# Gated cross-attention with routed experts on one core: stacks by single loads, softmax sums and reciprocals sent from GpSimd's program

## The reference

```python
# B = 8 batches, 256 tokens, 512 features, 32 query heads in 8 groups, head dim 16
q = X @ Wq.T + bq ; k = ctx @ Wk.T + bk ; v = ctx @ Wv.T + bv      # X = layernorm(x)
scores = einsum('bgrqd,bgkd->bgrqk', q, k) / sqrt(16)
scores = where(causal | padding, -inf, scores)
w = softmax(scores, axis=-1)
out = einsum('bgrqk,bgkd->bgrqd', w, v) ... @ Wo.T + bo
x = x + tanh(g_xattn) * out
# then a mixture of 8 experts (top 2 by a sigmoid gate + bias) and a shared expert:
x = x + tanh(g_ffn) * moe(layernorm(x))
```

## Time and profile before

| | before |
|---|---|
| device time, median of 3 runs | 839.02 us (834.45 to 839.38) |
| the profiled execution | 838.73 us; from first to last instruction (span) 836.8 us |
| PE busy | 695.0 us (83% of the span), 4417 matmuls |
| DVE / ACT / POOL busy | 452.3 / 290.4 / 109.3 us |
| mean granted TensorE clock | 0.884 of full |
| expert phase | from 648 us to the end |
| length of one full pass | about 68.3 us |

### The profile page before, as it was taken

The page is one execution under the profiler, slowest core; times in us unless marked ns, Lnnn a source line. Parts: engine busy times, 40 slices in busy tenths (PEclk is TensorE's granted clock), DMA queues, the critical chain, the costliest instruction groups (busy, mean ns, idle before and its releaser), DMA issues. The chain is left out here.

```text
span 836.8 us, 15086 instructions
## 1 busy us (share of the span) xinstructions
PE 695.0 (83%) x4417; PEld 481.2 (58%) x4417; DVE 452.3 (54%) x1017; ACT 290.4 (35%) x601; POOL 109.3 (13%) x132
## 2 busy tenths in 40 slices
PE   0345999899699799969979979989447999999998
PEld 0344757577477577758757758557236444444443
DVE  4517674467467556745736746634223455555554
ACT  1020454344344443433524434434210333333332
POOL 7400002102101210210210210110230000000000
PEclk9965978899899988988988989859667999999999
DMA  4785565455444643733644533421326012222211
GB/s 152 162 241 111 111 139 139 92 122 139 104 113 117 146 104 83 162 75 91 173 85 113 138 101 80 103 57 42 102 63 127 22 46 61 63 63 63 63 44 44
DMA packets 67696, 84.85 MB, mean 101 GB/s; under 512 B 15624, under 2 KB 44112, under 8 KB 67408
## 3 DMA queue, kind: packets, MB, share of 16 engines
q1 hardware_dynamic: 63504, 77.58, 36.4%
q0 software_dynamic: 2304, 6.29, 4.0%
q10 hardware_dynamic: 1856, 0.57, 0.3%
HBM read 60.48 MB, written 29.70 MB: 108 GB/s over the span
## 5 line engine op out<-in xcount | busy, mean ns | idle before, releaser
L623 ACT ACTIVATE probs<-ps 128x512 f32<-128x512 f32 x256 | 146.5, 598 | 153.1 <-PE ps L957 152.8
L831 DVE TENSOR_REDUCE mx<-ps 128x2 f32<-128x512 f32 x256 | 171.5, 683 | 47.2 <-PE ps L938 46.8
L1106 PE MATMUL ps_h<-w,q_sg 128*128 128x512 bf16 x512 | 132.9, 383 | 5.2 <-PEq L77 5.2
L938 PE MATMUL ps<-kst,qst 65*128 65x256 f32 x512 | 125.6, 331 | 12.9 <-DVE mx L831 7.7
L938 PEld LDWEIGHTS ps<-kst,qst 65*128 65x128 f32 x512 | 95.8, 211 | 61.9 <-issue 24.6
L957 PE MATMUL ps<-qst,kst 66*128 66x512 f32 x256 | 114.8, 450 | 5.2 <-DMA qst<-mrow 3.9
L1157 DVE SCALAR_TENSOR_TENSOR hid<-ps_h,sc_in,up 128x256 bf16<-128x256 f32 x128 | 61.9, 483 | 87.3 <-ACT up L1147 86.3
L1147 ACT ACTIVATE up<-ps_h,sc_in 128x256 f32<-128x256 f32 x128 | 60.7, 475 | 120.2 <-PE ps_h L1106 119.6
L1106 PEld LDWEIGHTS ps_h<-w,q_sg 128*128 128x128 bf16 x512 | 49.9, 99 | 67.8 <-issue 10.6
L970 PE MATMUL psa<-probs,v_st 128*32 128x256 f32 x1024 | 78.9, 432 | 1.2 <-ACT probs L623 1.2
L1124 PE MATMUL ps_o<-probs,hidT 128*128 128x512 bf16 x256 | 76.2, 380 | 0.8 <-DVE hidT L1163 0.8
(11 more groups left out here) (126 smaller groups left out, 1132.2 us busy)
## 6 DMA issues: line engine op xcount, KB each, us to landing
qst<-q_d SPq DMA_DIRECT2D x96, 128.0 KB
q_d<-q_sg SPq DMA_DIRECT2D x32, 256.0 KB, 2.2
a_d<-a_sb SPq DMA_DIRECT2D x32, 256.0 KB, 2.2
x_n<-in_x SPq DMA_DIRECT2D x8, 512.0 KB, 4.3
c_raw<-in_ctxT SPq DMA_DIRECT2D x8, 512.0 KB, 3.3
w<-in_w13T POOLq DMA_DIRECT2D x8, 512.0 KB, 16.0
a_dn<-a_d SPq DMA_DIRECT2D x16, 256.0 KB
a_lo<-r_d SPq DMA_DIRECT2D x16, 256.0 KB
```

The costliest lines, as they stand in the source:

```text
L623: act.activation(probs[:, v % 8, :], ps2[v % 2][:, :, :].rearrange("p h q -> p (h q)"), ACT.Exp, scale=HD ** -0.5).then_inc(s_exp, 1)
L831: dve.tensor_reduce(mx[:, c % 2, 0:8 * NT].rearrange("p (h t) -> p h t", t=NT)[:, h:h + 2, w // 2], ps1[u % 2][:, :, :], AX_X, ALU.max)\
L938: last = pe.matmul(o[:, i, :], qst[0:ROW_MAX, c, h, t * P:t * P + P], kst[0:ROW_MAX, c, g % 2, :], start=(i == 0 or not masked), stop=not ...
L1106: last = pe.matmul(o, xb[:, t, c, :], w13[:, e, c, :], start=(c == 0), stop=(c == DC - 1))
```

## The change

Single loads: `q_d` and `k_d` hold three rows per feature (hi, lo, hi and hi, hi, lo) and the padding row lies in `k_d`, so that each stack takes one load for q and one for k where it took seven; in turn each store becomes two, with half as many bytes again. Sums: `move_sums`, `store_r` and `load_r` are taken out of SP's program and issued from POOL's, in places of POOL's order; `normalise(b-1, 1)` goes ahead of `values(b+1, 0)`, and `residual_bias` ahead of `values(b, 3)`. Steps: Q1, Q2, Q3 move from 16, 18, 20 to 17, 20, 22, V0 and V1 from 21, 22 to 25, 26, and the second reciprocal with `load_values` from 20 to 19.

```diff
-PREP = [(11, "T0"), (12, "T1"), (13, "K"), (14, "Q0"), (16, "Q1"), (18, "Q2"), (20, "Q3"), (21, "V0"), (22, "V1")]
+PREP = [(11, "T0"), (12, "T1"), (13, "K"), (14, "Q0"), (17, "Q1"), (20, "Q2"), (22, "Q3"), (25, "V0"), (26, "V1")]
...
-        q_d = dram("q_d", (B, CH, P, 2, L))
-        k_d = dram("k_d", (B, P, 2, L))
-        pad_d = dram("pad_d", (B, L))
+        q_d = dram("q_d", (B, CH, P, 3, L))
+        k_d = dram("k_d", (B, G, HD + 1, 3, L))
...
             def store_k(nb, idx):
                 ready((s_free, idx["K"] + 1))
-                sp.dma_start(k_d[nb], f(k_sg[:, :, :])).then_inc(s_kw, 16)
+                kv = k_d[nb, :, 0:HD].rearrange("s d w q -> s d (w q)")
+                sp.dma_start(kv[:, :, 0:L], f(k_sg[:, hi, :])).then_inc(s_kw, 16)
+                sp.dma_start(kv[:, :, L:3 * L], f(k_sg[:, :, :])).then_inc(s_kw, 16)
...
-                sp.dma_start(q_d[nb, c], f(q_sg[:, c % 2])).then_inc(s_qw[c % 2], 16)
+                sp.dma_start(q_d[nb, c, :, 0:2], f(q_sg[:, c % 2])).then_inc(s_qw[c % 2], 16)
+                sp.dma_start(q_d[nb, c, :, 2], f(q_sg[:, c % 2, hi])).then_inc(s_qw[c % 2], 16)
...
-                for row, w in ((0, hi), (HD, lo), (2 * HD, hi)):
-                    sp.dma_start(f(qs[row:row + HD]), qv[w]).then_inc(s_stk[c], 16)
-                for row, w in ((0, hi), (HD, hi), (2 * HD, lo)):
-                    sp.dma_start(f(ks[row:row + HD]), kv[w]).then_inc(s_stk[c], 16)
-                sp.dma_start(f(ks[ROW_PAD:ROW_PAD + 1]), pad_d[bass.ds(nb, 1)].unsqueeze(1).broadcast_to([1, 2, L]))\
+                sp.dma_start(f(qst[0:ROW_PAD, c]), q_d[nb, c].rearrange("(s d) w q -> (d w) s q", d=HD))\
+                  .then_inc(s_stk[c], 16)
+                sp.dma_start(f(kst[0:ROW_PAD + 1, c]),
+                             k_d[nb, 2 * c:2 * c + 2].rearrange("s d w q -> (d w) s q")[0:ROW_PAD + 1])\
                   .then_inc(s_stk[c], 16)
...
             def body(b, attn, nxt, prev, old, base, par0):          # GpSimd's program
                 idx, _, at = numbered(attn, nxt, prev, old, base)
+                if prev:
+                    move_sums(b - 1, 1)
+                    store_r(b - 1, 0)
+                    load_r(b - 1, 0)
                 if attn:
                     values(b, 2, None)
+                if prev:
+                    move_sums(b - 1, 2)
                 if nxt:
                     deviation1(b + 1)
                 if prev:
                     normalise(b - 1, 0)
                     low_values(b - 1, 0)
+                if prev:
+                    residual_bias(b - 1)
                 if attn:
                     values(b, 3, None)
                 if prev:
-                    residual_bias(b - 1)
+                    move_sums(b - 1, 3)
+                    store_r(b - 1, 1)
+                    load_r(b - 1, 1)
+                    normalise(b - 1, 1)
+                    low_values(b - 1, 1)
+                if attn:
+                    move_sums(b, 0)
                 if nxt:
                     values(b + 1, 0, idx)
                 if prev:
-                    normalise(b - 1, 1)
-                    low_values(b - 1, 1)
                     deviation2(b - 1, 0)
                     deviation2(b - 1, 1)
...
-                    if u in (4, 20) and prev:
-                        h = u // 20
+                    if u in (4, 19) and prev:
+                        h = u // 19
```

More of the change, by code:

```diff
@@ L348, in store_a @@
                              a_sb[:, c % 2]).then_inc(s_aw[c % 2], 16)
-            def move_sums(b, c):
-                ready((s_aev, b * G + 2 * c + 2), (s_rd, b * 2 + c // 2 - 1))
-                for w in range(2):
-                    row = 32 * c + 16 * w
-                    sp.dma_start(den[row:row + 16, :], a_sb[HD:P:32, c % 2, w, :]).then_inc(s_den[c % 2], 16)
             def load_values(b, h):
@@ L363, in load_values @@
                              a_d[b, :, 0:HD, 2 * L * h:2 * L * h + 2 * L]).then_inc(s_ar[h], 16)
-            def store_r(b, h):
-                ready((s_rd, b * 2 + h + 1))
-                for i in range(2):
-                    c = 2 * h + i
-                    sp.dma_start(r_d[b, h, :, L * i:L * i + L], rden[32 * c:32 * c + 32, :]).then_inc(s_rw, 16)
-            def load_r(b, h):
-                ready((s_rw, b * 64 + 32 * h + 32), (s_ln2, b * LN2))
-                sp.dma_start(f(a_lo[:, 2 * h:2 * h + 2, :].rearrange("p c q -> p (c q)")),
-                             r_d[b, h].unsqueeze(1).broadcast_to([G, HD, 2 * L])).then_inc(s_rr[h], 16)
             def load_residual(b):
@@ L427, in body @@
                         c = {1: 1, 8: 2, 17: 3}[u]
-                        move_sums(b - 1, c)
                         store_a(b - 1, c)
@@ L442, in body @@
                         load_stack(b, 3)
-                    if prev and u in (5, 20):
-                        load_values(b - 1, u // 20)
-                    if prev and u in (5, 21):
-                        store_r(b - 1, u // 21)
-                    if prev and u in (9, 23):
-                        load_r(b - 1, u // 23)
+                    if prev and u in (5, 19):
+                        load_values(b - 1, u // 19)
                     if u == 17 and attn:
                         max_row(b, 1, idx)
-                    if nxt and u in (15, 17, 19, 21):
-                        store_q(b + 1, (u - 15) // 2, idx)
+                    if nxt and u in (15, 18, 21, 23):
+                        store_q(b + 1, {15: 0, 18: 1, 21: 2, 23: 3}[u], idx)
                     if nxt and u == 22:
@@ L455, in body @@
                     if attn and u == 24:
-                        move_sums(b, 0)
                         store_a(b, 0)
@@ L463, in _ @@
             passes(sp, body, prepare)
-            for s, n in ((s_kw, 16 * B), (s_rw, 64 * B),
-                         (s_qw[0], 32 * B), (s_qw[1], 32 * B), (s_aw[0], 32 * B), (s_aw[1], 32 * B)):
+            for s, n in ((s_kw, 32 * B),
+                         (s_qw[0], 64 * B), (s_qw[1], 64 * B), (s_aw[0], 32 * B), (s_aw[1], 32 * B)):
                 sp.wait_ge(s, n)
@@ L496, in values, with move_sums, store_r, load_r @@
                     .then_inc(s_vst, 1)
+            def move_sums(b, c):
+                ready((s_aev, b * G + 2 * c + 2), (s_rd, b * 2 + c // 2 - 1))
+                for w in range(2):
+                    row = 32 * c + 16 * w
+                    pool.dma_start(den[row:row + 16, :], a_sb[HD:P:32, c % 2, w, :]).then_inc(s_den[c % 2], 16)
+            def store_r(b, h):
+                ready((s_rd, b * 2 + h + 1))
+                for i in range(2):
+                    c = 2 * h + i
+                    pool.dma_start(r_d[b, h, :, L * i:L * i + L], rden[32 * c:32 * c + 32, :]).then_inc(s_rw, 16)
+            def load_r(b, h):
+                ready((s_rw, b * 64 + 32 * h + 32), (s_ln2, b * LN2))
+                pool.dma_start(a_lo[:, 2 * h:2 * h + 2, :].rearrange("p c q -> p (c q)").bitcast(F32),
+                             r_d[b, h].unsqueeze(1).broadcast_to([G, HD, 2 * L])).then_inc(s_rr[h], 16)
             def normalise(b, h):
@@ L558, in _ @@
             passes(pool, body, prepare)
+            pool.wait_ge(s_rw, 64 * B)
             pool.wait_ge(s_w13, 16 * E)
@@ L597, in item @@
                     act.wait_ge(s_item, n + 1)
-                    wait(act, s_qw[1], b * 32)
+                    wait(act, s_qw[1], b * 64)
                     act.activation(k_sg[:, hi, :], m[:, 0:L], ACT.Identity, bias=bk_c[:, 0:1]).then_inc(s_khi, 1)
@@ L602, in item @@
                     act.wait_ge(s_item, n + 1)
-                    wait(act, s_qw[c % 2], b * 32 + 16 * (c // 2))
+                    wait(act, s_qw[c % 2], b * 64 + 32 * (c // 2))
                     if c == 1:
-                        act.wait_ge(s_kw, b * 16 + 16)
+                        act.wait_ge(s_kw, b * 32 + 32)
                     act.activation(q_sg[:, c % 2, hi, :], m[:, 0:L], ACT.Identity, bias=bq_c[:, c:c + 1])\
```

11 lines of the change are left out of this document (4 added, 7 removed).

## The result

The changed kernel takes 858.08 us (median of 4 runs, 856.51 to 862.94) beside 839.2 us before: a ratio of 1.0246, 95% interval 1.0189 to 1.0304. It is slower by 19 us where 27 us less were forecast, and 26 us above the upper end of the range. The profiled execution's span is 857.4 us (before: 836.8), the mean granted clock 0.875 (before: 0.884).

A forecast was written before the change was run, and what follows sets the result against it. PE was taken to bound the pass, with idle time and lost clock at W0 to win. From 838.7 us, 28 off for five full passes, 2.4 off for the start and 3.6 added for the drain gave 811.9, forecast 812; range 788 to 832.

The forecast's parts named there:

- PE's way to W0: Full passes: PE reaches W0 at 220 to 221, where it came at 221.2, leaving a wait of 2 to 3 us.
- A new wait earlier in the pass: norm1 on DVE waits 1.5 us for POOL's deviation1, now behind chunk 2's sums; 0.8 us a pass reaches PE (0 to 1.5).
- Single loads in the passes: Full passes: they free SP of 20 issues a pass and add five; worth nothing, as PE waited for no stack.
- The start: Before the first scores: two issues replace seven, so the first stack's issues end 2.7 us sooner; 2.4 us won (0 to 2.7).
- The chain: Second half's sums to W0 in a full pass: 16.3 us (14.5 to 17.8) in place of 21.4, W0 4.3 us earlier.
- The price of a hop from POOL: Each of the chain's three transfers costs 0.6 us more from POOL than from SP (bounds 0 and 1.1).
- The clock at W0: Half of W0's 2.56 us lost to half speed comes back with the shorter wait: 1.3 us per full pass.
- Rival B: Hops cost 1.1 us and W0 still runs at half speed: 827 us; chance 0.14.
- The drain: After the last pass: sums leave 2.8 us later, store_r 1.8 later, three hops at 0.6; 3.6 us lost (1.8 to 5.1).
- The slower side: Chance 0.06 that the changed kernel is slower; with hops 2.5 us dearer than SP's it would take 853 us.
- Rival D: DVE's stops at norm1 and the reciprocal bring PE to W0 4 us later; only clock is won: 827 or 833 us; chance 0.13.
- The forecast's list of signs: Wrong if POOL's hops land over 1.7 us later, row-maxima waits exceed 2 us a pass, or a stack is waited for.

The follow-up runs named there:

- a4_dev: The changed kernel with deviation1 moved ahead of chunk 2's sums in POOL's order: 840.5 us, ratio 1.0052 to the kernel before.
- d1_pool_dev: c2 with deviation1 moved ahead of chunk 2's sums in POOL's order: 818.8 us, ratio 0.9825 to the kernel before.
- c1_stk_steps: The kernel before with the new steps and the single loads, sums and reciprocals still issued from SP: 842.9 us, ratio 1.0149.
- e1_regk_dev: The changed kernel with deviation1 ahead of chunk 2's sums and k_d in even rows, padding row apart: 824.0 us, ratio 0.9868 to the kernel before.
- c2: The kernel before with the new steps and POOL's transfers, stacks still in seven loads: 843.3 us, ratio 1.0139.
- e2: d2 with the next batch's first stack issued by SP at step 25 in place of 22: 803.6 us, ratio 0.9622 to the kernel before.
- c4: The kernel before with the new steps and SP's queue reordered, load_r ahead of the next stack, no transfers from POOL: 823.6 us, ratio 0.9891.
- d2: d1_pool_dev with residual_bias between the second half's sums' issue and store_r: 814.5 us, ratio 0.9791 to the kernel before.
- d4: c4 with only load_r issued from POOL: 830.1 us, ratio 0.9933 to the kernel before.
- e3: e2 with the eight loads of the experts' first weights moved from before pass 0 into pass 1: 797.5 us, ratio 0.9508 to the kernel before.
- c3: The changed kernel with k_d in 128 even rows and the padding row in its own buffer and load: 847.0 us, ratio 1.0164 to the kernel before.

## Why the prediction was wrong, point by point

**PE's way to W0.** The forecast's sum rests on PE reaching W0 when it did before, or 1 us sooner (220 to 221), and on a chain 5 us shorter that begins 0.8 us later. Measured from the DVE instruction that reads the W of the batch before, over passes 2 to 6: PE stood ready for W0 after 56.8 us before and after 61.8 now. The sums left after 42.4 us and now leave after 45.8. From the sums to W0 the chain went from 20.2 to 19.2 us in the mean (the 21.4 of pass 2, from which I had worked, was its longest). So it shrank by 1 us and began 3.3 us later, and W0 starts 2.3 us later in each pass in place of 4.3 sooner. The step that failed is the cost of what happens earlier in the pass, in its two terms:

**A new wait earlier in the pass: the term that failed most.** DVE's wait was rightly seen, 2.28 us where I had 1.5. Its price to PE was put at 0.8 us a pass, 4 in all. Undone, it gave 17.6 us (a4_dev) and 24.5 (d1_pool_dev), of which an estimated 14 to 17 are the clock's. Three things were left out: the first `norm1` becomes longer beside POOL (0.53 to 1.48 us); the transposes on PE wait for it at once, so that being two buffers ahead covers nothing; and the clock falls behind the gap of 2 us, the largest part. I had counted the clock's price for W0's gap and for no other. And a fourth: `residual_bias`, moved ahead, meets DVE's L756 and costs PE 1.54 us a pass.

**Single loads in the passes: costed at nothing.** They cost 13.5 us on top of the steps (c1_stk_steps), and even rows alone gave 16.5 back (e1_regk_dev). I asked who waits for a stack's load, found nobody, and stopped. The stores had changed too, and who waits for those stood in the earlier trace rows: Q1, 2.84 us, for k's store. Q1 at step 17 gave it one step of room, and the gapped rows used up more (6.6 us in place of 4.1).

**The start: 2.4 us gained, 10.6 lost.** The two issues in place of seven were right, 0.8 us in all (64.01 to 64.84), and worth nothing, since the stores ahead of them landed later. About 3 to 4 us come with the single loads and their stores, in full queues; the rest arises between the first scores and batch 0's W, by the norm wait and k's store (e1 is back at 165.6). I had named the bytes and given them 0.3 us.

**The chain: 16.3 us forecast, 19.0 measured.** `residual_bias` in front and W0's wait of about 3 us came as written. The price of a hop from POOL, 0 to 1.1 us, was the right answer to the wrong question. For `load_r` it is 0 within what the rows show (3.65 and 3.8 us from POOL, 4.2 and 4.3 from SP, each with no stack beside it). In the drain, where the whole chain can be compared, it took 15.05 us from POOL (620.22 to 635.27) and 15.5 from SP (598.46 to 613.96): the sums 2.1 us longer, with six loads of the expert phase issued right behind them, the other two hops 1.2 and 0.6 us shorter. Whether those loads or POOL made the sums longer was not tried. The forecast also took all three hops for small transfers; the page of the kernel before lists `a_lo<-r_d` with 256 KB, the other two with 4 and 8. What lengthens `load_r` is a stack issued beside it, 6.0 to 6.4 us from either engine. In the changed kernel SP issued the stack at 297.53 and 297.98 and POOL `load_r` at 298.06; it was used at 304.47. The change took `load_r` out of SP's queue, and by this freed SP to issue the stack at that very moment. I had taken three durations from the drain, where no stack is loaded. The Trainium skill ("DMA: Bandwidth & Descriptors", section "Specifications") has the first byte of GpSimd's path later by 0.4 us; no run here shows such a difference for these transfers.

**The clock at W0.** Half of 2.56 us was counted as gain. 2.56 was the worst pass: over passes 2 to 6 W0 took 4.3 to 5.3 us before, 4.9 in the mean, so its clock cost 2.1. After, with waits of 2.87 to 3.75, it took 4.4 to 5.1. So next to nothing of it came back; the window of W0 in pass 3 of the changed kernel shows 0.57:

```profile
307.60:311.60 4.00, 3.80 (x10) 3.02 (x11) 0.00 (x0) 0.05 (x1) 1.49 (x4) 0.57 0.02 2
```

Rival B had this right: a gap of 3 us was enough here. In c2, d1 and e2 W0 ran at the full clock behind ten of eleven waits of 0.9 to 1.9 us, behind one of two at 2.4 us, and behind none of 2.7 us and more. But before the transposes of c2 1.8 us were enough, so the gap's length alone doesn't decide.

**The drain**: 3.6 us lost was forecast; PE's longest wait is 18.3 in place of 17.2, and the last distance between two W 55.0 us in place of 54.4. The hops were priced at 1.8 us and cost nothing.

**The rivals.** The slower side was given 0.06, all of it to dear hops, and that mechanism is refuted. Rival D came nearest: DVE's stop at `norm1` holds back PE, which comes to W0 5 us later than before (D said 4 later than the forecast). But it let this take at most W0's gain, since it counted PE's new gaps as moved ones at full clock, and it kept the chain's start in its place. Its second stop, at the reciprocal, cost PE nothing that the rows of pass 3 show. The forecast's list of signs named PE's waits for row maxima, of more than 2 us a pass; in a full pass they came to 1.85 us (1.54 and 0.31), and those for `x_n`, which it didn't name, to 2.0. The mechanism at W0 was right: beyond the steps, c4 won 6.5 us and e2 26.5 by a shorter chain; the order in which the change realises it spoiled it.

## What to carry to other kernels

When transfers move into another engine's in-order program, ask of every instruction that then stands behind them who waits for it, and price that wait with the clock it costs, not only with its length. When a load is made simpler by a store of another form, look for who waits for the store. When a transfer leaves a queue, look at what the queue will issue in its place: the load on the critical chain should have the time behind it free, and large loads without haste belong where no chain is running.

## What the runs showed of the hardware that I had not expected

**DVE beside POOL.** DVE's product of 128x16 elements (L756), 0.17 us for others of its size, took 2.30 us, from 286.43 to 288.73, while POOL's `residual_bias` ran from 286.33 to 288.70. Of the two `norm1` of a pass, the one beside POOL's `normalise` took 1.48 us and the other 0.53; in d1, with `deviation1` ahead of the sums, all four of passes 2 and 3 took 0.53. The Trainium skill ("SBUF — State Buffer", section "Who interferes with whom") says that DVE and GpSimd share a pair of ports as an exclusive lock, for the length of an instruction; L756, which reads two operands from SBUF, ended when POOL's instruction did, which agrees. Moving POOL's work moves the place: in d1 the 128x16 instruction L747, 0.16 us elsewhere, took 1.24 us, 254.03 to 255.27, beside `normalise` (253.93 to 255.22).

**What is issued beside a transfer.** The same load of reciprocals takes 3.65 to 4.3 us with no stack beside it and 6.0 to 6.4 with a stack's loads issued close to it, behind it (c4: 212.75 and 214.46; d1: 211.57 and 212.41) or from 2.2 us ahead of it (d2: 213.92 and 211.72; the changed kernel: 298.06 and 297.53). By the lists of transfers its median from issue to landing is 5.5 to 6.5 us in the changed kernel, c2, d1 and d2, and 3.7 to 3.9 in d4, e2 and e3. With the stack's loads of q 3 to 4 us ahead of it, it is back at 3.8 (before: 216.07 and 220.32, used 224.09). Bytes alone don't explain it: in the drain before, about 770 KB of the expert phase's loads were issued from 0.7 us behind it, and it was used after 4.2. Six us behind the last of 4 MB of weights, the sums took 16.5 us.

**Rows with gaps.** A store of 256 KB into evenly spaced rows, with 128 KB beside it, landed in about 2 us by the list of transfers (c3, e1; alone it took 2.0 us in d1 and 4.1 before); the pair with a gap behind every 16 rows held its buffer for 6.6 us, and its issues took 0.7 us in place of 0.33.

**Gaps and the clock.** 1.8 us without work on PE were followed by 8 us at 0.60 and 0.55 in c2. Between the profiled executions of c2 and d1, 22 of 28 us of span were PE's busy time. And the clock fell to the same level without any gap: behind the gate's 24 matmuls of 128x8 in d1, 8 us at 0.59 and 0.55, and at the same item in every full pass of the kernel before.
